# B of the state-space scan goes by DRAM and GpSimd, and the decays go to PSUM, in an eight-sequence sandwich kernel

## The chip, the cores and the metric

One core of a Trainium2 chip runs the whole kernel. The metric is device time in microseconds (us) of one execution; lower is better. Engines are TensorE (PE), VectorE (DVE), ScalarE (ACT), GpSimd (POOL) and SyncE (SP, which issues the DMAs here). Each works through its own instructions in order and waits on semaphores.

## What is computed

Eight sequences of 512 tokens, 256 wide, pass through two layers: attention, a routed mixture of eight small experts, a selective state-space block, and a ternary-weight feed-forward block, with norms and residual adds between them. The change touches the state-space block. For each of 512 inner channels and 16 states it runs a recurrence over the 512 tokens:

```
x, B, C, delta = projections of the hidden state
dA    = exp(delta * A)               # the decay, one per channel, state and token
state = dA * state + (delta * u) * B # B of a group of channels, state and token
y     = sum over the 16 states of state * C
```

B is shared by groups of 128 channels (64 rows in all: 4 groups of 16 states); C has 512 rows, one for every 16 channels and each state.

## The kernel before

**Staging.** Every sequence goes through three chains of steps: `early` (attention, gate), `late` (experts, norms, the projections of the state-space block, delta and du = delta * u), and, after the scan, `back` (gate by z, output projection, feed-forward block, store). The scan of a sequence has 64 tiles of 128 channels by 512 tokens, `PER = 64`: four channel tiles `ct` times 16 states `st`. An iteration runs the scan of sequence s and, woven into it, `late` of s+1, `early` of s+2 and `back` of s-1. The first iteration has no `back` chain of an earlier sequence, the second to last no `early`, and the last neither `early` nor `late`. A prologue with the first sequences' chains and an epilogue with the last `back` chain lie around the eight iterations.

**Order.** The order of each engine's work is fixed when the program is written out. `iteration` walks over steps j = -1 to 67 with three parts each (`SLOTS`), calls the scan function of the engine for (j, part), and then emits the chain steps that `in_slots` put into that slot; it spreads each chain's rounds by the planner's costs (`COST`). Within an engine nothing overtakes: a chain step that waits holds the scan work behind it.

**The scan of tile n in before** is made of these instructions, named by function:
- `scan_act`, part 0 of step n-1 (line 919): ScalarE writes decay(n) = exp(delta * a) into one of `NDA = 4` SBUF buffers, after scan n-4.
- `scan_pe`, part 1 of step n-1 (line 743): TensorE multiplies a one-hot selector (`sel_b`) by `b_rows` (B in three bf16 parts that add up to fp32) to spread row n of B over 128 partitions, into one of two PSUM banks `ps_b` (`NDB = 2`), after scan n-2.
- `scan_dve`, part 1 of step n (line 1210): VectorE multiplies that bank by du, in place.
- `scan_dve`, part 0 of step n+1 (line 1203): VectorE runs the recurrence, state(n) from decay and `ps_b`, into one of three state buffers (`NS = 3`), after product n-3.
- `scan_pool`, part 0 of step n+2 (line 1226): GpSimd multiplies state(n) by C from `c_all`, into one of four `prod` buffers.
- `scan_pe`, part 2 of step n+3 or n+4 (line 750): TensorE adds the product into `ps_y` by an identity matmul; after 16 tiles VectorE takes y out (line 1216).
- `scan_sync` (line 1308): one DMA of 256 KB for each tile loads C rows from DRAM, each row repeated over 16 partitions, into one of `NC = 5` buffers.

**Preparing B in before** (chain `late`): `bm` (24 small matmuls), `b_hi`, `b_rest`, `b_mid`, `b_lo` (ten VectorE instructions that split B into three bf16 parts), `b_turn` (8 transposes), `b_turned` (one ScalarE copy). x has a projection of its own, `xs`. C goes through `c`, `c_out`, `c_store` into DRAM.

Of the kernel before, what the change touches and what calls it, by code (L numbers as in the profile page):

```python
# [5 lines left out]
F32 = mybir.dt.float32  # L6
# [5 lines left out]
P = 128  # L12
# [36 lines left out]
C_BANK, CONV_BANK, D_BANK = (2, 1, 2, 0), (0, 2, 1, 0), (2, 1, 0, 2)  # L49
# [104 lines left out]
def late_rounds():  # L154

    steps = []
    for i in range(MCH):
        at, routed = 3 * i, i >= MCH - RCH
        steps += [(at, "P", ("up1", i)), (at + 1, "A", ("tanh", i)), (at + 1, "P", ("up3", i)), (at + 2, "V", ("silu", i))]
        if routed:  # L160
# [5 lines left out]
    steps = [(0, "P", "dt"), (0, "P", "bm"), (0, "V", "x4_zero"), (1, "A", "dt_out"), (1, "V", "b_hi"), (1, "P", ("c", 0)),  # L166
             (2, "V", "b_rest"), (2, "A", ("c_out", 0)), (3, "V", "b_mid"), (3, "P", ("c", 1)), (3, "S", ("c_store", 0)),
             (4, "V", "b_lo"), (4, "A", ("c_out", 1)), (4, "P", ("c", 2)), (5, "P", "b_turn"), (5, "A", ("c_out", 2)),
             (5, "S", ("c_store", 1)), (6, "A", "b_turned"), (6, "S", ("c_store", 2)), (6, "P", "xs"),
             (7, "P", ("c", 3)), (7, "A", ("x4", 0)), (8, "A", ("c_out", 3)),  # L170
             (9, "S", ("c_store", 3)), (9, "A", ("x4", 1)), (9, "P", ("conv", 0)),
             (10, "P", ("conv", 1)), (11, "P", ("conv", 2)), (13, "P", ("conv", 3))]
    for i in range(CT):
        steps += [(10 + i + (i == 3), "A", ("x_tanh", i)), (11 + i + (i == 3), "A", ("x_one", i)),
                  (12 + i + (i == 3), "V", ("u", i))]
    d0 = (14, 15, 17, 18)
# [38 lines left out]
def quant_rounds():  # L215
# [20 lines left out]
    "h_turned": 12, "dt": 15, "bm": 15, "dt_out": 7, "b_turn": 6, "b_turned": 12, "c": 15, "c_out": 7, "xs": 15, "x4": 24,  # L236
# [46 lines left out]
def sandwich(nc, base, wqT, bq, wkT, b_k, wvT, bv, woT, bo, gateT, gate_b, w1T, w3T, w2T, winT, wdtT, b_dt,  # L283
             conv_w, conv_b, a_log, d_param, woutT, w_fc, w_proj, ident, tri, sel_e, sel_n, out):
    c_rows = nc.dram_tensor("c_rows", [2, CT, P, T], F32).ap()
    ctx = ExitStack()
    with ctx:  # L287
# [26 lines left out]
        sel_b = sb("sel_b", [P, NST, 1], BF16)  # L314
# [12 lines left out]
        xn = sb("xn", [P, NT, D], BF16)  # L327
# [5 lines left out]
        b_rows = sb("b_rows", [P, 2, 2, T], BF16)  # L333
# [4 lines left out]
        NC, NDA, NDB, NS, NP = 5, 4, 2, 3, 4  # L338
        c_all = sb("c_all", [P, NC, T])
        decay = sb("decay", [P, NDA, T])  # L340
# [34 lines left out]
        bp = view(arena_l, 512, [NT, 2, 2, 64], BF16)  # L375
        br = view(arena_l, 1024, [NT, 64])
# [18 lines left out]
        win_f = c_all[:].rearrange("p a t -> p (a t)").rearrange("p (k n) -> p k n", k=KD)  # L395
# [27 lines left out]
        ps_b = ctx.enter_context(nc.psum_tensor("ps_b", [P, 2, T], F32))  # L423
# [11 lines left out]
        c_stored = [sem(f"c_stored{i}") for i in range(2)]  # L435
        out_stored = sem("out_stored")

        b_spread = sem("b_spread")
# [5 lines left out]
        y_taken = sem("y_taken")  # L444
        c_spread = [sem(f"c_spread{i}") for i in range(8)]
# [17 lines left out]
        ATTN_N, GATE_N, MOE_N, SSM_N = 8, 5, 4, 5  # L463
# [140 lines left out]
        def late_pe(eng, s, step):  # L604
# [38 lines left out]
            elif name == "bm":  # L643
                for t in range(NT):
                    n = 0
                    for part in range(3):
                        for k in range(KD):
                            ins = nc.tensor.matmul(ps_x[:, 1, t * 64:(t + 1) * 64],
                                                   hT[:, s.par, k, t * P:(t + 1) * P], win[:, k, part, BC:BC + 64],
                                                   start=(n == 0), stop=(n == 5))  # L650
                            n += 1
            elif name == "c":
                if i == 1:
                    eng.wait_ge(late["V"], la(s, "V", "b_rest"))
                elif i == 2:
                    eng.wait_ge(late["A"], la(s, "A", ("c_out", 0)))
                elif i == 3:
                    eng.wait_ge(late["A"], la(s, "A", "b_turned"))
                ins = project(ps_x[:, C_BANK[i], :], CC + i * P, P, hT[:, s.par])
            elif name == "b_turn":  # L660
                eng.wait_ge(late["V"], la(s, "V", "b_lo"))
                eng.wait_ge(late["A"], la(s, "A", "dt_out"))
                for pair in range(2):
                    for t in range(NT):
                        ins = nc.tensor.transpose(
                            xb(0)[:, pair * T + t * P:pair * T + (t + 1) * P],
                            bp[:, t, pair, :, :].rearrange("p a b -> p (a b)"), idb[:])
            elif name == "xs":
                eng.wait_ge(late["A"], la(s, "A", ("c_out", 1)))
                ins = project(ps_x[0:NXB * NST, 1, :], XC, NXB * NST, hT[:, s.par])  # L670
            elif name == "conv":
                if i == 0 and is_seq(s, 0):
                    eng.wait_ge(ready_conv, 1)
                eng.wait_ge(late["A"], la(s, "A", (("c_out", 3), ("c_out", 2), ("x4", 1), ("x4", 1))[i]))
                if i < 2:
                    eng.wait_ge(late["A"], la(s, "A", ("x4", 0)))
                elif i == 3:
                    eng.wait_ge(late["V"], la(s, "V", ("u", 0)))
# [56 lines left out]
        def scan_pe(eng, s, j, part):  # L735
            n = j + 1
            if part == 1 and 0 <= n < PER:
                if n == 0:
                    eng.wait_ge(late["A"], la(s, "A", "b_turned"))
                wait(eng, scanned, s.count(PER, n + 1 - NDB))  # L740
                ct, st = n // NST, n % NST
                lo = 64 * (ct % 2)
                nc.tensor.matmul(ps_b[:, n % NDB, :], sel_b[lo:lo + 48, st, :].broadcast_to([48, P]),  # L743
                                 b_rows[lo:lo + 48, s.par, ct // 2, :], start=True, stop=True).then_inc(b_spread, 1)
            if part == 2:
                for n in sums_at(j):
                    if n % NST == 0:
                        wait(eng, y_taken, s.count(PER, n))
                    eng.wait_ge(multiplied, s.count(PER, n + 1))
                    nc.tensor.matmul(ps_y[:], idf[:], prod[:, n % NP, :], start=(n % NST == 0),  # L750
                                     stop=(n % NST == NST - 1)).then_inc(reduced, 1)
# [60 lines left out]
        def late_act(eng, s, step):  # L812
# [21 lines left out]
            elif name == "b_turned":  # L834
                eng.wait_ge(late["P"], la(s, "P", "b_turn"))
                wait(eng, b_spread, s.count(PER, -PER))
                ins = nc.scalar.copy(b_rows[:, s.par], xb(0).rearrange("p (k t) -> p k t", k=2))
# [4 lines left out]
            elif name == "x4":  # L842
                eng.wait_ge(late["P"], la(s, "P", "xs"))
# [200 lines left out]
        def late_dve(eng, s, step):  # L1044
# [25 lines left out]
            elif i == "add":  # L1070
                eng.wait_ge(late["A"], la(s, "A", ("m", "apply")))
                wait(eng, back["G"], s.count(BPER, BACK_AT["G"][("w", "add")] - 2 * BPER))
                ins = tt(x2[:, s.par], x1[:, s.par], xn[:], ALU.add)
            elif name in ("silu", "weighted", "gated"):
# [11 lines left out]
                else:  # L1086
                    own(("silu" if shared else "weighted", i))
                    eng.wait_ge(late["P"], la(s, "P", ("up3", i)))
                    if i == 0:
                        for k in range(2):  # L1090
                            wait(eng, c_stored[k], s.count(PER, 0))
                    if shared:
# [6 lines left out]
            elif name == "b_hi":  # L1099
                eng.wait_ge(late["P"], la(s, "P", "bm"))  # L1100
                ins = nc.vector.tensor_copy(b_part(0), b_psum())
            elif name == "b_rest":
                own("b_hi")
                for t in range(NT):
# [518 lines left out]
```

## Time and profile before

| | us |
|---|---|
| time, median of 3 runs | 2097.96 (2095.51 to 2100.2) |
| the profiled execution's own time | 2099.33 |
| its span (first to last instruction) | 2097.5 |
| busy: PE / DVE / ACT / POOL | 1651.5 / 1770.0 / 1035.9 / 913.8 |

The page groups instructions by source line: busy time, count and mean duration, then how long the engine sat idle just before them and what ended that. Such idle time counts only where the engine is the one that sets the pace. A table of stretches gives the busy time of each engine in windows of the span, with the clock that TensorE was granted and the share of time that the 16 DMA engines were busy.

### The profile page before, as it was taken

What the parts mean: (1) busy time and instruction counts of PE and PEld (TensorE: products, weight loads), DVE (VectorE), ACT (ScalarE), POOL (GpSimd) and SP (SyncE); (2) the same over time, 40 slices, a digit from 0 to 9 for tenths busy, and PEclk for the clock granted to TensorE, in tenths of its full rate; (3) what the DMA queues carried; (4) which work ended last, traced back from release to release, by engine and by line L of the source; (5) the groups of instructions that cost most, each with busy time, mean ns of one, the idle gap of its engine ahead of it and who ended that gap; (6) DMA issues with size and microseconds to landing.
All of it is one profiled execution on the core that took longest, in us unless ns stands there. A gap on an engine that the chain in (4) does not pass through costs nothing. (4 is left out here: it accounts for less than half of the span.)

```text
span 2097.5 us, 22567 instructions
## 1 busy us (share of the span) xinstructions
PE 1651.5 (79%) x5875; PEld 725.3 (35%) x5948; DVE 1770.0 (84%) x3142; ACT 1035.9 (49%) x1745; POOL 913.8 (44%) x676
## 2 busy tenths in 40 slices
PE   3375577778996889868997799878997899779856
PEld 1122123232452335322452335332452335234324
DVE  6577899989879998979989998999989987987830
ACT  3247444825555454735556355734547344734312
POOL 0101534454437434554346434464346544665510
PEclk9977699979997999979997899979997899999978
DMA  4100222222222222222231222222222223223300
GB/s 108 46 0 21 72 79 89 92 69 77 75 92 65 85 71 86 85 67 78 74 101 65 81 76 76 96 75 72 76 96 71 76 85 106 86 99 113 110 10 11
DMA packets 94601, 157.95 MB, mean 75 GB/s; under 512 B 10940, under 2 KB 23660, under 8 KB 94468
## 3 DMA queue, kind: packets, MB, share of 16 engines
q1 hardware_dynamic: 94468, 156.43, 22.9%
q8 instruction: 52, 0.85, 0.2%
q14 instruction: 81, 0.66, 0.1%
HBM read 143.83 MB, written 12.58 MB: 75 GB/s over the span
## 5 line engine op out<-in xcount | busy, mean ns | idle before, releaser
L1226 POOL TENSOR_TENSOR prod<-state,c_all 128x512 f32<-128x512 f32 x512 | 669.6, 1312 | 706.8 <-DVE state L1203 644.0
L1203 DVE TENSOR_TENSOR_SCAN state<-decay,ps_b 128x512 f32<-128x512 f32 x512 | 619.7, 1210 | 9.7 <-issue 0.4
L750 PE MATMUL ps_y<-prod,idf 128*128 128x512 f32 x1024 | 610.6, 689 | 4.8 <-DVE u L1216 3.6
L1210 DVE TENSOR_TENSOR ps_b<-du,ps_b 128x512 f32<-128x512 f32 x512 | 347.7, 679 | 87.3 <-PE ps_b L743 86.8
L919 ACT ACTIVATE decay<-delta,a_neg 128x512 f32<-128x512 f32 x512 | 359.3, 719 | 32.3 <-DVE state L1203 29.3
L743 PE MATMUL ps_b<-b_rows,sel_b 48*128 48x512 bf16 x512 | 209.9, 411 | 155.0 <-DVE state L1203 152.7
L750 PEld LDWEIGHTS ps_y<-prod,idf 128*128 128x128 f32 x1024 | 183.8, 207 | 136.3 <-issue 109.9
L743 PEld LDWEIGHTS ps_b<-b_rows,sel_b 48*128 48x128 bf16 x512 | 47.8, 94 | 467.3 <-DVE state L1203 332.5
L619 PE MATMUL ps_x<-xT,w 128*128 128x512 bf16 (+1 forms) x391 | 132.0, 422 | 80.1 <-DVE arena_l L1095 65.6
L826 ACT ACTIVATE arena_l<-ps_x 128x512 f32<-128x512 f32 (+1 forms) x104 | 61.8, 594 | 190.8 <-PE ps_x L619 189.7
L535 PE MATMUL ps_x<-hT,win 128*128 128x512 bf16 (+1 forms) x455 | 135.6, 441 | 21.4 <-DVE arena_b L1171 16.6
L722 PE MATMUL ps_x<-arena_b,fcT 128*128 128x512 f32 x256 | 130.5, 634 | 6.0 <-ACT arena_b L901 4.8
L727 PE MATMUL ps_x<-pjT,arena_b 128*128 128x256 f32 x512 | 118.2, 384 | 3.1 <-ACT arena_b L907 1.7
L727 PEld LDWEIGHTS ps_x<-pjT,arena_b 128*128 128x128 f32 x512 | 95.3, 190 | 23.6 <-issue 6.4
L619 PEld LDWEIGHTS ps_x<-xT,w 128*128 128x128 bf16 (+1 forms) x416 | 32.4, 102 | 180.8 <-DVE arena_l L1095 104.9
L535 PEld LDWEIGHTS ps_x<-hT,win 128*128 128x128 bf16 (+1 forms) x480 | 48.5, 109 | 107.7 <-issue 44.3
L890 ACT ACTIVATE arena_b<-ps_x 128x512 f32<-128x512 f32 x32 | 19.0, 593 | 125.1 <-PE ps_x L535 125.1
L781 ACT ACTIVATE arena_e<-arena_e 128x512 bf16<-128x512 bf16 x64 | 39.6, 620 | 76.4 <-DVE arena_e L984 76.4
L901 ACT ACTIVATE arena_b<-ps_x 128x512 f32<-128x512 f32 x64 | 38.4, 599 | 75.0 <-PE ps_x L722 75.0
L1081 DVE SCALAR_TENSOR_TENSOR arena_l<-arena_l,ps_x 128x512 f32<-128x512 f32 (+1 forms) x104 | 69.9, 672 | 6.4 <-ACT arena_l L826 5.9
L711 PE MATMUL ps_x<-wout,u 128*128 128x256 f32 x256 | 61.9, 397 | 16.0 <-DVE u L1175 13.4
L722 PEld LDWEIGHTS ps_x<-arena_b,fcT 128*128 128x128 f32 x256 | 48.7, 200 | 65.4 <-issue 48.6
(230 smaller groups left out, 2422.2 us busy)
## 6 DMA issues: line engine op xcount, KB each, us to landing
c_all<-c_rows SPq DMA_DIRECT2D x512, 256.0 KB
c_rows<-arena_l SPq DMA_DIRECT2D x32, 256.0 KB
out<-arena_b SPq DMA_DIRECT2D x8, 512.0 KB
x_in<-in_base SPq DMA_DIRECT2D x8, 256.0 KB
c_all<-in_winT SPq DMA_DIRECT2D x1, 1280.0 KB, 7.5
arena_b<-in_w_fc SPq DMA_DIRECT2D x1, 1024.0 KB, 5.7
arena_b<-in_w_proj SPq DMA_DIRECT2D x1, 1024.0 KB, 5.0
w<-in_w1T SPq DMA_DIRECT2D x1, 792.0 KB, 5.9
```

What stands on the lines that cost most here:

```text
L535: ins = nc.tensor.matmul(dst, win[:, k, part, lo:lo + n], rhs[:, k, :], start=(i == 0), stop=(i == 5))
L619: ins = nc.tensor.matmul(ps_x[0:m, bank, :], w[:, k, c * P:c * P + m], xT[:, k, :], start=(k == 0), stop=(k == KD - 1))
L711: ins = nc.tensor.matmul(half_bank(XB, t), u[:, s.par, ct, t * P:(t + 1) * P], wout[:, ct, :], start=(ct == 0), stop=(ct == CT - 1))
L722: ins = nc.tensor.matmul(ps_x[:, XB, :], fcT[:, k, i * P:(i + 1) * P], x3T[:, k, :], start=(k == 0), stop=(k == KD - 1))
L727: ins = nc.tensor.matmul(ps_x[:, XB, 0:D], hf[:, m, i * P:(i + 1) * P], pjT[:, m, :], start=(m == 0), stop=(m == FM - 1))
L743: nc.tensor.matmul(ps_b[:, n % NDB, :], sel_b[lo:lo + 48, st, :].broadcast_to([48, P]), b_rows[lo:lo + 48, s.par, ct // 2, :], start=True, ...
L750: nc.tensor.matmul(ps_y[:], idf[:], prod[:, n % NP, :], start=(n % NST == 0), stop=(n % NST == NST - 1)).then_inc(reduced, 1)
L919: nc.scalar.activation(decay[:, n % NDA, :], delta[:, slot(s, ct), :], ACT.Exp, scale=a_neg[:, ct, st:st + 1]).then_inc(decayed, 1)
L1081: ins = stt(g, g, 1.0, ps_x[0:m, 0, :], ALU.add, ALU.mult)
L1203: nc.vector.tensor_tensor_scan(state[:, n % NS, :], decay[:, n % NDA, :], ps_b[:, n % NDB, :], 0.0, ALU.mult, ALU.add).then_inc(scanned, 1)
L1210: nc.vector.tensor_tensor(ps_b[:, j % NDB, :], du[:, slot(s, ct), :], ps_b[:, j % NDB, :], ALU.mult).then_inc(driven, 1)
L1226: nc.gpsimd.tensor_tensor(prod[:, n % NP, :], state[:, n % NS, :], c_all[:, n % NC, :], ALU.mult).then_inc(multiplied, 1)
```

## The change

**B** is projected together with x (`xb`, 128 rows in one go), ScalarE halves its 64 rows into an SBUF buffer (`b_out`), and one DMA stores them to a DRAM tensor `b_rows` (`b_store`). In the scan SyncE issues a second 256 KB load for each tile: one 2 KB row repeated over 128 partitions into one of `NB = 4` buffers `b_all`. GpSimd multiplies it by du into one of `NDB = 4` SBUF buffers `drive`, in step n-1, ahead of its product of tile n-3. The TensorE spread (line 743), the VectorE multiply (line 1210), `bm`, the five-step split, `b_turn`, `b_turned` and `xs` are gone.

**The decays** go from ScalarE into two PSUM banks (`NDA = 2`, before 4 in SBUF), so decay n waits for scan n-2. C has `NC = 4` buffers instead of 5, and its loads are issued from two steps on. The rounds of the last part of `late` are placed anew, the delta steps three rounds earlier.

```diff
-C_BANK, CONV_BANK, D_BANK = (2, 1, 2, 0), (0, 2, 1, 0), (2, 1, 0, 2)
+C_BANK, CONV_BANK, D_BANK = (2, 0, 2, 1), (0, 2, 1, 0), (2, 1, 0, 2)
...
+    steps = [(0, "P", "dt"), (0, "P", "xb"), (0, "V", "x4_zero"), (1, "A", "dt_out"), (1, "A", "b_out"), (1, "P", ("c", 0)),
+             (2, "P", ("c", 1)), (2, "S", "b_store"), (2, "A", ("c_out", 0)), (3, "A", ("x4", 0)), (3, "P", ("c", 2)),
...
-    d0 = (14, 15, 17, 18)
+        at = (6, 8, 10, 12)[i]
+        steps += [(at, "A", ("x_tanh", i)), (at + 1, "A", ("x_one", i)), (at + 2, "V", ("u", i))]
+    d0 = (11, 13, 15, 16)
...
-        NC, NDA, NDB, NS, NP = 5, 4, 2, 3, 4
-        c_all = sb("c_all", [P, NC, T])
-        decay = sb("decay", [P, NDA, T])
+        NB, NC, NDA, NDB, NS, NP = 4, 4, 2, 4, 3, 4
+        bc_all = sb("bc_all", [P, NB + NC, T])
+        b_all, c_all = bc_all[:, 0:NB], bc_all[:, NB:NB + NC]
+        drive = sb("drive", [P, NDB, T])
...
-        ps_b = ctx.enter_context(nc.psum_tensor("ps_b", [P, 2, T], F32))
+        decay = ctx.enter_context(nc.psum_tensor("decay", [P, NDA, T], F32))
...
+            elif name == "xb":
+                ins = project(ps_x[:, 1, :], XC, 2 * NXB * NST, hT[:, s.par])
...
         def scan_pe(eng, s, j, part):
-            n = j + 1
-            if part == 1 and 0 <= n < PER:
-                if n == 0:
-                    eng.wait_ge(late["A"], la(s, "A", "b_turned"))
-                wait(eng, scanned, s.count(PER, n + 1 - NDB))
-                ct, st = n // NST, n % NST
-                lo = 64 * (ct % 2)
-                nc.tensor.matmul(ps_b[:, n % NDB, :], sel_b[lo:lo + 48, st, :].broadcast_to([48, P]),
-                                 b_rows[lo:lo + 48, s.par, ct // 2, :], start=True, stop=True).then_inc(b_spread, 1)
...
+            elif name == "b_out":
+                eng.wait_ge(late["P"], la(s, "P", "xb"))
+                ins = act(bs[NXB * NST:P, :], ps_x[NXB * NST:P, 1, :], ACT.Copy, scale=0.5)
...
-                nc.vector.tensor_tensor_scan(state[:, n % NS, :], decay[:, n % NDA, :], ps_b[:, n % NDB, :], 0.0,
+                nc.vector.tensor_tensor_scan(state[:, n % NS, :], decay[:, n % NDA, :], drive[:, n % NDB, :], 0.0,
                                              ALU.mult, ALU.add).then_inc(scanned, 1)
-            if part == 1 and 0 <= j < PER:
-                ct = j // NST
-                if j % NST == 0:
-                    eng.wait_ge(late["G"], la(s, "G", ("du", ct)))
-                eng.wait_ge(b_spread, s.count(PER, j + 1))
-                nc.vector.tensor_tensor(ps_b[:, j % NDB, :], du[:, slot(s, ct), :], ps_b[:, j % NDB, :],
-                                        ALU.mult).then_inc(driven, 1)
...
         def scan_pool(eng, s, j, part):
+            n = j + 1
+            if part == 0 and 0 <= n < PER:
+                ct = n // NST
+                if n % NST == 0:
+                    eng.wait_ge(late["G"], la(s, "G", ("du", ct)))
+                eng.wait_ge(b_spread[n % 8], s.count(2 * PER, 16 * (n // 8 + 1)))
+                wait(eng, scanned, s.count(PER, n + 1 - NDB))
+                nc.gpsimd.tensor_tensor(drive[:, n % NDB, :], du[:, slot(s, ct), :], b_all[:, n % NB, :],
+                                        ALU.mult).then_inc(driven, 1)
...
+            if step == "b_store":
+                eng.wait_ge(late["A"], la(s, "A", "b_out"))
+                wait(eng, driven, s.count(PER, -PER))
+                eng.dma_start(b_rows[s.par], bs[NXB * NST:P, :]).then_inc(b_stored, PER)
+                return
...
-            for n in range(NC) if j == -1 else [j + NC - 1] if 1 <= j <= PER - NC else []:
+            for n in range(NB) if j == -1 else [j + NB] if 0 <= j < PER - NB else []:
                 stored = counted(eng, s.count(PER, PER)) if n == 0 else None
-                used = counted(eng, s.count(PER, n - NC + 1 if n >= NC else 0))
+                used = counted(eng, s.count(PER, n - NB + 1))
+                if n == 0:
+                    eng.wait_ge(b_stored, stored)
+                wait(eng, driven, used)
+                eng.dma_start(b_all[:, n % NB, :], b_rows[s.par, n:n + 1, :].broadcast_to([P, T])).then_inc(b_spread[n % 8], 16)
+            for n in range(NC) if j == -1 else [j + NC - 3] if 3 <= j <= PER - NC + 2 else []:
+                stored = counted(eng, s.count(PER, PER)) if n == 0 else None
+                used = counted(eng, s.count(PER, n - NC + 1))
```

## Rows read from the trace of the kernel before

**Rows 1.** Stretches by iteration: first, longest and shortest full one, last two.
```profile
231.50:452.70 221.20, 166.62 (x536) 60.53 (x546) 210.86 (x347) 109.66 (x181) 106.21 (x78) 0.86 0.25 84
...
690.80:932.70 241.90, 198.21 (x728) 89.04 (x737) 216.55 (x388) 127.43 (x217) 114.50 (x84) 0.92 0.24 80
...
1168.30:1403.90 235.60, 201.56 (x730) 89.51 (x739) 217.55 (x386) 127.35 (x217) 114.54 (x84) 0.91 0.24 80
...
1641.40:1849.50 208.10, 182.55 (x612) 79.79 (x618) 177.60 (x266) 105.65 (x171) 104.45 (x80) 0.94 0.27 88
1849.50:2002.70 153.20, 136.89 (x407) 59.89 (x407) 134.07 (x176) 61.48 (x101) 87.93 (x69) 0.97 0.33 111
```

**Rows 2.** The page's costliest groups: busy, mean ns of one, idle before, releaser.
```profile
L1226 POOL TENSOR_TENSOR prod<-state,c_all 128x512 f32<-128x512 f32 x512 | 669.6, 1312 | 706.8 <-DVE state L1203 644.0
L1203 DVE TENSOR_TENSOR_SCAN state<-decay,ps_b 128x512 f32<-128x512 f32 x512 | 619.7, 1210 | 9.7 <-issue 0.4
...
L1210 DVE TENSOR_TENSOR ps_b<-du,ps_b 128x512 f32<-128x512 f32 x512 | 347.7, 679 | 87.3 <-PE ps_b L743 86.8
L919 ACT ACTIVATE decay<-delta,a_neg 128x512 f32<-128x512 f32 x512 | 359.3, 719 | 32.3 <-DVE state L1203 29.3
L743 PE MATMUL ps_b<-b_rows,sel_b 48*128 48x512 bf16 x512 | 209.9, 411 | 155.0 <-DVE state L1203 152.7
```

**Rows 3.** Stretches of one full iteration, eight scan tiles each (columns as Rows 1).
```profile
1168.30:1195.70 27.40, 23.88 (x84) 10.60 (x83) 27.36 (x54) 12.66 (x22) 15.41 (x11) 0.94 0.25 84
1195.70:1223.40 27.70, 22.04 (x66) 7.63 (x66) 27.66 (x47) 13.44 (x24) 11.13 (x9) 0.88 0.23 77
1223.40:1251.00 27.60, 24.63 (x80) 9.48 (x80) 27.45 (x44) 16.43 (x32) 10.28 (x8) 1.00 0.25 76
1251.00:1280.50 29.50, 27.89 (x116) 14.03 (x116) 25.88 (x45) 17.31 (x33) 11.48 (x9) 1.00 0.23 75
1280.50:1307.20 26.70, 24.54 (x141) 15.68 (x144) 20.72 (x42) 13.34 (x23) 11.58 (x9) 1.00 0.24 80
1307.20:1335.00 27.80, 27.64 (x117) 14.86 (x117) 23.60 (x58) 13.99 (x25) 11.20 (x9) 1.00 0.35 111
1335.00:1363.20 28.20, 21.36 (x70) 7.03 (x68) 27.90 (x49) 23.62 (x40) 15.89 (x12) 0.87 0.22 74
1363.20:1403.90 40.70, 29.59 (x65) 10.19 (x67) 36.97 (x57) 16.56 (x23) 27.59 (x17) 0.67 0.21 66
```

**Rows 4.** Timeline of VectorE and GpSimd, 655 to 660 us: start, duration, instruction.
```profile
655.62 0.42 DVE L1121 TENSOR_SCALAR arena_l<-arena_l 128x512 f32<-128x512 f32 x1
...
657.15 1.27 POOL L1226 TENSOR_TENSOR prod<-state,c_all 128x512 f32<-128x512 f32 x1
657.69 0.68 DVE L1210 TENSOR_TENSOR ps_b<-du,ps_b 128x512 f32<-128x512 f32 x1
658.27 0.69 DVE L1175 TENSOR_TENSOR u<-u,arena_b 128x512 f32<-128x512 f32 x1
658.37 1.72 POOL L1248 TENSOR_TENSOR delta<-du,delta 128x512 f32<-128x512 f32 x1
658.88 1.76 DVE L1124 TENSOR_TENSOR arena_l<-arena_l 128x512 f32<-128x512 f32 x1
```

**Rows 5.** Two VectorE groups of the full iteration, columns as Rows 2.
```profile
L1121 DVE TENSOR_SCALAR arena_l<-arena_l 128x512 f32<-128x512 f32 x4 | 4.5, 1128 | 0.0
...
L1117 DVE SCALAR_TENSOR_TENSOR u<-ps_x,cb,u 128x512 f32<-128x512 f32 x4 | 2.9, 730 | 0.0
```

**Rows 6.** Three of GpSimd's 14 other groups of that iteration, columns as Rows 2.
```profile
L1248 POOL TENSOR_TENSOR delta<-du,delta 128x512 f32<-128x512 f32 x4 | 5.9, 1473 | 0.6 <-DVE du L1128 0.6
...
L1234 POOL TENSOR_TENSOR sd_x<-vb_x,hf 128x4 bf16<-128x4 bf16 x1 | 1.0, 1019 | 9.2 <-DVE vb_x L946 9.2
...
L509 POOL TENSOR_TENSOR rs_o<-ve_o,mhalf 128x4 f32<-128x4 f32 x1 | 1.0, 1007 | 3.9 <-DVE ve_o L1160 3.9
```

**Rows 7.** DMA issues: a load of 256 KB, median us from issue to landing.
```profile
wdt<-in_wdtT SPq DMA_DIRECT2D x1, 256.0 KB, 4.6
```

## What the change will do to the time, predicted before any run of it

> **What bounds the kernel now.** I read the table of stretches first, by iteration [rows 1]. Its columns are the stretch and its length, then the busy time of PE, weight loads, DVE, ACT and POOL, the granted TensorE clock, the DMA share and GB/s. The five full iterations take 235.6 to 241.9 us, and VectorE is busy for 217 of them, TensorE for 201, GpSimd for only 115. So VectorE is the pace, TensorE is close behind, and GpSimd is half idle. The last iteration is short, 153.2 us, because it has no early and late chains.
>
> Next the groups by line [rows 2]: per tile VectorE spends 1.210 us on the scan and 0.679 on the multiply by du, and nearly all of its idle time there (87.3 us) is ended by the TensorE spread of B, which itself waits for the scan two tiles back. GpSimd's product takes 1.312 us on average, nearly twice VectorE's time for the same form.
>
> Last, one full iteration cut into eight stretches of eight tiles [rows 3]. In stretches 1, 2, 3 and 7 VectorE is busy all the time (27.66 of 27.70). In 4 to 6 TensorE is (27.64 of 27.80). In the eighth nobody is full (36.97 of 40.70): it holds the delta steps, the gate and the passage to the next iteration. The busier of VectorE and TensorE sums to 227.5 us over the eight, against 235.6 measured: the in-order coupling costs 3.6%.
>
> **Part 1, VectorE loses the multiply.** Start to start it costs 0.58 us (657.69 to 658.27 [rows 4]; records overlap by 0.1), so 8 x 0.58 = 4.6 us per stretch and 37 per iteration. The split of B goes too (ten short instructions, about 3 us per iteration, in the late chain), and so does the wait for the spread, about 10 us per iteration; both are inside the stretch lengths, so I count them only through the maxima below. The same instruction exists only on GpSimd afterwards.
>
> **Part 2, GpSimd gains it.** The form is the one of its product: two fp32 SBUF inputs, 128x512. Back to back these cost 1.22 us (657.15 to 658.37 [rows 4]). Two of them per tile make 19.5 us per stretch and 156 per iteration. Its other work is its busy time less 8 x 1.31: 4.9, 0.6, 0, 1.0, 1.1, 0.7, 5.4 and 17.1 us in the eight stretches, 31 in all [rows 2, 3].
>
> **Part 3, the two engines exclude each other.** VectorE's multiply of two SBUF tensors at 658.88 took 1.76 us where its like took 0.69: GpSimd's instruction ran until 660.09, and VectorE ended 0.55 later. GpSimd's own, started at 658.37, took 1.72 instead of 1.27 behind VectorE's SBUF multiply of 658.27 [rows 4]. L1121 with a single SBUF source took 0.42 once and 1.128 on average [rows 5]. Instructions with a PSUM operand are not held, in either order of the operands: L1117, PSUM first and SBUF second, takes 730 ns evenly, like L1210 [rows 2, 5]. The new scan has this order too (decay in PSUM, drive in SBUF), so I leave it at 1.21; bounds 1.21 and, if it were held like the rest, 1.9. By the code a full iteration has about 93 VectorE instructions without a PSUM operand that are fit to be held, about 25 of them in the last stretch. GpSimd is busy half the time now and nearly always afterwards. I take 0.2 us more for GpSimd per such instruction (free durations 0.3 to 0.7, less overlap, less those that meet no one), 19 per iteration, 9 of it in the last stretch and 1.4 in each other; for VectorE 18 more waiting than now, 6 and 1.7. Bounds: 0 and twice that.
>
> The Trainium skill (SBUF — State Buffer, section "SBUF: two separate sides") puts this as an exclusive lock for the whole instruction. Taken to the letter, 128 full durations of 1.27 plus 31 plus some 30 of held VectorE work is 224 us of one port per iteration before any coupling, some 6 more than my sum. The trace agrees that they exclude each other, but back-to-back GpSimd instructions start every 1.22.
>
> **Part 4, TensorE** loses 8 x 0.411 = 3.3 us per stretch [rows 2] and some matmuls of the B preparation, which I count at nothing.
>
> **Part 5, ScalarE.** Decay n now waits for scan n-2, so it has one step (some 3.3 us) for 0.719 us of work [rows 2]. Behind it queue all chain steps of ScalarE; they come no earlier than the scan of their step. Cover: ScalarE is busy 127 of 236 us. Nothing for it; if every decay were exposed, 46 us per iteration. A write to PSUM instead of SBUF: no row, bounds -0.1 and +0.1 us, hidden.
>
> **Part 6, DMA.** C's loads keep the 16 DMA engines 0.24 busy [rows 1], that is 0.9 us per tile; B adds as much. B's load for tile n+4 may start when drive n is done and is wanted four steps later, some 13 us; a 256 KB load landed 4.6 us after its issue [rows 7]. C has one buffer fewer but still four steps. Hidden, and the b_store too, since B leaves far ahead of delta. On SyncE both loads stand in one queue with the chains' stores; a late store delays both by what it waits, with some 8 us of slack.
>
> **The sum for a full iteration**, largest of GpSimd (19.5 + other + held), VectorE (busy - 4.6 + held) and TensorE (busy - 3.3) [rows 3]: 25.8 (GpSimd), 24.8 (VectorE), 24.6 (VectorE), 24.6 (TensorE), 22.0 (GpSimd), 24.3 (TensorE), 26.3 (GpSimd), 45.6 (GpSimd: 19.5 + 17.1 + 9). That is 218.0 where it was 227.5. With 4% of coupling it gives 226.7 against 235.6: -8.9, five times -45. First iteration, with the lighter mix: -5. Second to last: GpSimd 156 + 21 + 8 = 185, plus its idle passage, about 200 against 208.1: -8. **Last iteration**: VectorE would need only about 100, but GpSimd 156 + 8 + 5 = 169, with coupling 173 against 153.2: +20. Prologue: -1. Together -39: 2099.3 - 39 = 2060 for the profiled execution, which lies 1.4 above the median of the runs; I predict 2060.
>
> **Rivals.**
> 1. *GpSimd turns into the pace and its waits come with it: slower.* GpSimd runs 13 chain instructions in an iteration (roots, deltas, adds) in order with drive and product. Its 14 other groups have 33 us of idle time before them now, from L1248's 0.6 to rs_o's 3.9 with sd_x's 9.2 between [rows 6]. Half idle, it doesn't feel them. If they stay, a full iteration needs 156 + 31 + 19 + 33 = 239 us, 3 more than the 235.6 now. Five of these make +15, the last iteration adds its +20, the first and the second to last stay: +35, 2134. It decides from about 20 us of such waits per iteration. For: in-order, and many waits for VectorE. Against: VectorE may run two steps ahead of a late GpSimd, so most predecessors will be done.
> 2. *TensorE's clock.* It was granted 1.00 (2.4 GHz) in the full stretches 4 to 6 and 0.67 in the last, where it was busy 29.59 of 40.70 us (a mix of both levels) [rows 3]. With 3.3 us less per stretch more of them may be granted less; then stretches 4 to 6 stay at 27.6 and the gain of 8 to 9 us per full iteration is gone: 2100. The Trainium skill's page TensorE: Matmul & The Clock Gate (section "HAM oscillation — how this bites in real kernels") describes a clock that is cut when the matmul stream pauses, and so speaks for this one.
> 3. *Loads late.* If one DRAM row read 128 times is slow (C reads eight rows), each tile waits; at 1 us a tile +512 us less the slack, at least 2200. No releaser of L1226 is a DMA now [rows 2].
> 4. *Couplings vanish*, as VectorE no longer waits for the spread: the full iterations come to 218, 17.6 less, total -88 - 13 + 18: 2015.
> That the change does not do what it says is not open: the instructions are in the diff.
>
> **How the numbers follow.** Forecast 0.50, rival 1 0.28, rival 2 0.09, rival 3 0.04, rival 4 0.09. The forecast's own range, from held time 0 to double (19 per full iteration either way, damped by VectorE-bound stretches to about 6), is 2025 to 2098. Range for 8 in 10: 2010 to 2135. No change is what a measurement cannot tell from 2098, within 0.2%, 4 us. Faster: 0.46 of the forecast, rival 4 and a third of rival 2, 0.58. Same: 0.03 of the forecast, 0.04 of rival 2 and 0.03 of rival 1, 0.10. Slower: the rest, 0.32.
>
> **What would show it.** GpSimd busy over 200 of a full iteration; VectorE near 190; the last iteration near 173 us and full of GpSimd; the scan at 1.21 us still; VectorE's SBUF instructions longer (L1121 over 1.2 us); no wait of GpSimd for a DMA. It would be wrong if GpSimd idles over 20 us per full iteration waiting for VectorE (rival 1), if the scan is longer than 1.3 us, or if ScalarE's decay is what the scan waits for.

## The result, and the profile after

The changed kernel takes 2110.64 us (median of 7 runs, 2104.84 to 2121.6); the kernel before takes 2098.19 (2095.51 to 2100.28). The ratio is 1.0064, 95% interval 1.004 to 1.0088: slower by 0.6%, where I forecast 2060, faster by 1.8%. The measured time lies in the range that I gave, and the sign is wrong. The profiled execution took 2104.84 us with a span of 2103.0; it is the fastest of the seven, so the trace shows 5.5 of the 12.5 us between the medians.

The page's groups that answer to [rows 2] (busy us, mean ns, idle before, releaser):

```profile
L1177 POOL TENSOR_TENSOR prod<-state,bc_all 128x512 f32<-128x512 f32 x512 | 673.6, 1316 | 165.9 <-DVE state L1152 143.8
L1152 DVE TENSOR_TENSOR_SCAN state<-decay,drive 128x512 f32<-128x512 f32 x512 | 618.6, 1211 | 91.9 <-POOL prod L1177 64.8
...
L1170 POOL TENSOR_TENSOR drive<-du,bc_all 128x512 f32<-128x512 f32 x512 | 670.2, 1310 | 10.9 <-issue 5.5
L887 ACT ACTIVATE decay<-delta,a_neg 128x512 f32<-128x512 f32 x512 | 352.4, 691 | 633.2 <-DVE state L1152 624.4
```

The scan still takes 1.211 us, and the multiply, now on GpSimd, 1.310. New are the 633 us that ScalarE idles before its decays, nearly all of it waiting for the scan; before it was 32.3 us.

The stretches that answer to [rows 1]: first iteration, the five full ones together, second to last, last. Columns: stretch, length, busy PE, weight loads, DVE, ACT, POOL, granted clock, DMA share, GB/s. First the kernel before, whose five full iterations did not stand in one row yet, then the changed one.

```profile
452.70:1641.40 1188.70, 1007.43 (x3647) 449.19 (x3695) 1084.20 (x1919) 636.97 (x1085) 572.60 (x420) 0.91 0.24 78
```

```profile
228.50:450.20 221.70, 142.54 (x447) 56.34 (x446) 193.76 (x274) 112.45 (x183) 185.98 (x143) 0.80 0.54 164
450.20:1647.20 1197.00, 897.73 (x3215) 440.17 (x3214) 1045.30 (x1548) 653.88 (x1095) 979.58 (x741) 0.86 0.49 149
1647.20:1841.90 194.70, 156.79 (x523) 77.37 (x521) 142.79 (x192) 106.63 (x171) 182.17 (x144) 0.92 0.58 179
1841.90:2011.70 169.80, 123.72 (x347) 58.99 (x348) 110.58 (x114) 62.88 (x102) 161.98 (x131) 0.86 0.62 189
```

Where the 5.5 us come from: the five full iterations +8.3 (239.4 us each, before 237.7), the last +16.6, the second to last -13.4, the prologue -3.0, the epilogue -3.5, the first +0.5. The two last iterations came out near the forecast (+20 and -8). The full iterations, where I had expected -45, gained nothing, although neither VectorE (209.1 us each, 87%) nor GpSimd (195.9, 82%) nor TensorE (179.5, 75%) is full.

One full iteration of the changed kernel in eight stretches of eight scan tiles, columns as above, to be set beside [rows 3]:

```profile
1176.90:1207.50 30.60, 23.16 (x79) 11.31 (x78) 28.83 (x47) 12.92 (x22) 22.84 (x19) 0.89 0.45 134
1207.50:1233.10 25.60, 17.72 (x58) 6.71 (x57) 24.43 (x39) 13.65 (x24) 23.55 (x19) 0.93 0.55 166
1233.10:1260.90 27.80, 23.01 (x77) 9.40 (x76) 27.61 (x37) 16.63 (x32) 20.77 (x17) 1.00 0.52 156
1260.90:1289.00 28.10, 23.27 (x99) 13.49 (x100) 22.87 (x37) 17.36 (x33) 21.44 (x17) 0.88 0.53 153
1289.00:1314.40 25.40, 25.40 (x132) 17.27 (x131) 16.72 (x28) 12.62 (x23) 20.70 (x17) 1.00 0.54 165
1314.40:1336.30 21.90, 20.58 (x90) 12.66 (x89) 21.27 (x46) 14.73 (x25) 20.40 (x16) 1.00 0.68 217
1336.30:1368.00 31.70, 19.35 (x70) 8.02 (x68) 26.73 (x41) 22.74 (x35) 26.26 (x21) 0.87 0.47 148
1368.00:1412.50 44.50, 23.20 (x48) 7.69 (x49) 38.51 (x48) 20.00 (x28) 39.99 (x26) 0.63 0.39 115
```

In stretches 4, 7 and 8 no engine is full: 28.10 us with 23.27 of the busiest, 31.70 with 26.73, 44.50 with 39.99.

So the account of VectorE is what has to be explained. Per full iteration it was busy 216.8 us and idle 20.9; it is now busy 209.1 and idle 30.3. The multiply and the split took 40 away, so 177 were to be expected before any longer holding: **busy is 32 us above that**. And the idle time changed hands. Its waits in the five full iterations, first of the kernel before, then of the changed one (us in total, times, longest):

```profile
DVE ps_b L1210 <- PE ps_b L743: 51.7, 36, 4.1
DVE st_m L497 <- PE ps_x L633: 18.2, 10, 3.0
DVE u L1216 <- PE ps_y L750: 18.1, 5, 3.8
```

```profile
DVE g L965 <- ACT g L771: 24.2, 5, 4.8
DVE arena_e L937 <- ACT arena_e L759: 23.7, 5, 4.8
DVE arena_e L945 <- ACT arena_e L746: 21.7, 10, 3.1
DVE arena_b L1120 <- ACT arena_b L858: 15.7, 5, 3.2
DVE state L1152 <- ACT decay L887: 14.5, 10, 1.9
...
DVE arena_l L1049 <- ACT arena_l L795: 9.8, 10, 3.4
...
DVE state L1152 <- POOL prod L1177: 5.0, 5, 1.2
```

For TensorE it waits 4.8 us per iteration instead of 17.6, for ScalarE 22.2 instead of 0.8. All rows of ScalarE but the `decay` row are waits for **chain steps** of ScalarE, not for the decays. For GpSimd VectorE waits only 1.2 us per iteration.

Both can be seen in one place, in the 1176.9 to 1412.5 iteration (start, duration, engine, instruction):

```profile
1181.67 4.08 DVE L919 TENSOR_SCALAR arena_e<-x_in,mb_x 128x256 bf16<-128x256 bf16 x4
1185.67 1.21 DVE L1152 TENSOR_TENSOR_SCAN state<-decay,drive 128x512 f32<-128x512 f32 x1
```

```profile
1181.95 1.26 POOL L1170 TENSOR_TENSOR drive<-du,bc_all 128x512 f32<-128x512 f32 x1
1183.18 1.26 POOL L1177 TENSOR_TENSOR prod<-state,bc_all 128x512 f32<-128x512 f32 x1
1184.41 1.26 POOL L1170 TENSOR_TENSOR drive<-du,bc_all 128x512 f32<-128x512 f32 x1
```

```profile
1181.41 0.69 ACT L887 ACTIVATE decay<-delta,a_neg 128x512 f32<-128x512 f32 x1
1186.92 0.69 ACT L887 ACTIVATE decay<-delta,a_neg 128x512 f32<-128x512 f32 x1 [4.82 <-DVE state L1152]
1187.55 0.58 ACT L795 ACTIVATE arena_l<-ps_x 128x512 f32<-128x512 f32 x1
```

Four short norm instructions of VectorE, free 0.27 us each, take 4.08 us together: 0.41 the first, 1.30 each of the others. GpSimd has its next instruction ready at each turn here, and the two engines alternate: one norm instruction, one GpSimd instruction. GpSimd isn't slowed by it, its instructions still start every 1.23 us. The scan behind them starts only at 1185.67; ScalarE's next decay waits for it, 4.82 us; and the chain step behind the decay, the tanh of L795, comes only then.

This is the worst case, not the rule. Of the 30 such bursts of four in the five full iterations, 14 had three or four instructions held (over 0.9 us each), nine had one or two, and seven none. Together the bursts take 19.1 us per full iteration, where the kernel before has 9.1, so they are 10 of the 32 us. Nor is it always GpSimd that wins. In the kernel before, at the same place:

```profile
1173.06 1.98 DVE L951 TENSOR_SCALAR arena_e<-x_in,mb_x 128x256 bf16<-128x256 bf16 x4
```

```profile
1171.32 3.64 POOL L1226 TENSOR_TENSOR prod<-state,c_all 128x512 f32<-128x512 f32 x2
```

Here three norm instructions pass at 0.27 us each while the second product, started at 1172.54, takes 2.42 us instead of 1.27; only the fourth is held (1.39). What decides who is first is not shown.

### The profile page after: what moved, and what is told of

Its sections match the earlier page's. It is cut to its first block and busy times, and to the rows that moved or that the text cites. A ratio compares the mean times of both kernels' runs of the same rounds, so it can differ in the third digit from the quotient of the medians.

```text
span 2103.0 us, 22040 instructions
## 1 busy us (share of the span) xinstructions
PE 1473.4 (70%) x5180; PEld 706.9 (34%) x5180; DVE 1652.5 (79%) x2550; ACT 1056.6 (50%) x1757; POOL 1555.2 (74%) x1188
## 5 line engine op out<-in xcount | busy, mean ns | idle before, releaser
L1177 POOL TENSOR_TENSOR prod<-state,bc_all 128x512 f32<-128x512 f32 x512 | 673.6, 1316 | 165.9 <-DVE state L1152 143.8
L1152 DVE TENSOR_TENSOR_SCAN state<-decay,drive 128x512 f32<-128x512 f32 x512 | 618.6, 1211 | 91.9 <-POOL prod L1177 64.8
L1170 POOL TENSOR_TENSOR drive<-du,bc_all 128x512 f32<-128x512 f32 x512 | 670.2, 1310 | 10.9 <-issue 5.5
L719 PEld LDWEIGHTS ps_y<-prod,idf 128*128 128x128 f32 x1024 | 204.4, 217 | 326.3 <-POOL prod L1177 183.7
L533 PE MATMUL ps_x<-hT,win 128*128 128x512 bf16 x480 | 142.9, 447 | 102.7 <-DVE arena_b L1120 93.4
L533 PEld LDWEIGHTS ps_x<-hT,win 128*128 128x128 bf16 x480 | 49.6, 109 | 207.6 <-DVE arena_b L1120 119.0
L795 ACT ACTIVATE arena_l<-ps_x 128x512 f32<-128x512 f32 (+1 forms) x104 | 61.1, 587 | 51.0 <-PE ps_x L617 50.7
L1188 POOL TENSOR_TENSOR g<-g,half 128x32 f32<-128x32 f32 x8 | 45.7, 5712 | 28.9 <-DVE g L975 28.9
L709 PEld LDWEIGHTS ps_x<-arena_b 128*128 128x128 f32 x512 | 61.8, 192 | 9.3 <-issue 8.1
L1053 DVE TENSOR_TENSOR arena_l<-arena_l,ps_x 128x512 f32<-128x512 f32 x88 | 59.1, 671 | 4.5 <-PE ps_x L625 2.5
L709 PE MATMUL ps_x<-arena_b 128*128 128x128 f32 x512 | 62.3, 275 | 0.0
```

The costliest lines, as they stand in the source:

```text
L533: ins = nc.tensor.matmul(dst, win[:, k, part, lo:lo + n], rhs[:, k, :], start=(i == 0), stop=(i == 5))
L709: ins = nc.tensor.matmul(ps_x[:, XB, D:D + P], hf[:, m, i * P:(i + 1) * P], hf[:, m, i * P:(i + 1) * P], start=(m == 0), stop=(m == FM - 1))
L1152: nc.vector.tensor_tensor_scan(state[:, n % NS, :], decay[:, n % NDA, :], drive[:, n % NDB, :], 0.0, ALU.mult, ALU.add).then_inc(scanned, 1)
L1170: nc.gpsimd.tensor_tensor(drive[:, n % NDB, :], du[:, slot(s, ct), :], b_all[:, n % NB, :], ALU.mult).then_inc(driven, 1)
L1177: nc.gpsimd.tensor_tensor(prod[:, n % NP, :], state[:, n % NS, :], c_all[:, n % NC, :], ALU.mult).then_inc(multiplied, 1)
```

## The experiments

Three theories. **A:** the two decay buffers hold ScalarE's chain steps behind the scan. **B:** GpSimd and VectorE exclude each other instruction by instruction, so bursts of short VectorE instructions pay a whole GpSimd instruction each. **C:** TensorE's lower granted clock (0.857, before 0.899) eats the gain, rival 2 of the prediction.

Ratios are to the kernel before, measured beside each group of runs. Its median was 2094.86 to 2098.99 us there and the changed kernel was measured only with the first, so differences in us between medians of different groups can be off by some 4 us.

### e1 and e4: ScalarE's decay is emitted later

```diff
         def scan_act(eng, s, j, part):
             n = j + 1
-            if part == 0 and 0 <= n < PER:
+            if part == 2 and 0 <= n < PER:
```

> Changed kernel with ScalarE's decay of tile n emitted in part 2 of step n-1 instead of part 0, so that its wait for scan n-2 holds fewer chain steps of ScalarE. Theory A (the two PSUM buffers tie ScalarE to the scan, its chain steps come late and VectorE waits for them, 22 us of idle time per full iteration): VectorE's idle time ended by ScalarE falls from 22 to under 10 us per full iteration, and the time from 2110 to 2030 to 2060. Theory B (the port that GpSimd and VectorE share costs the time, VectorE is longer busy): idle time moves into lock time or waits for GpSimd, 2095 to 2110.

Measured: 2082.26 us, ratio to before 0.9931 (0.9914 to 0.9948), 28 us under the changed kernel and 0.7% under the kernel before. e4 puts the decay yet one part later (`n = j`, part 0):

> Changed kernel with ScalarE's decay of tile n emitted in part 0 of step n instead of step n-1 (one part later than in e1), where scan n-2 is always done before. Theory A: ScalarE no longer waits for the scan at all (76 us of its idle time per full iteration in the changed kernel, 40 in e1, now under 15) and its chain steps come in time; 2060 to 2080. Against it: the scan of tile n has only one step for its decay, and VectorE's waits for the decay itself (2.9 us per full iteration, 5.5 in e1) grow; if these win, 2085 to 2110.

Measured: 2079.12 us, 0.9931 (0.991 to 0.9953), the same as e1. The full iterations fall from 239.4 to 233.7 (e1) and 234.7 us (e4):

```profile
446.80:1615.50 1168.70, 891.57 (x3215) 438.56 (x3214) 1050.53 (x1549) 648.71 (x1095) 978.20 (x741) 0.86 0.49 153
```

VectorE's busy time is unchanged (210.1 each), its idle time falls by 6.7. The time is less than expected of theory A, and so is the cause: VectorE waits for ScalarE still 17 us per full iteration in e1, where I had expected under 10. ScalarE's own wait before the decays (whole run; changed kernel, e1, e4):

```profile
ACT decay L887 <- DVE state L1152: 624.4, 340, 8.8
```
```profile
ACT decay L887 <- DVE state L1152: 374.2, 204, 11.6
```
```profile
ACT decay L887 <- DVE state L1152: 273.1, 136, 8.8
```

The held time falls, but even in e4 it is 29 us per full iteration (76 in the changed kernel, 40 in e1), where I had expected under 15. My reading, which no run tests, is that ScalarE, busy 129 of 235 us, catches up with VectorE wherever the decay stands. The price of the shift shows too: the scan waits more for the decay itself, 37.6 us in e1 and 53.3 in e4, 26.9 in the changed kernel.

### e2: the kernel before with two decay buffers

```diff
-        NC, NDA, NDB, NS, NP = 5, 4, 2, 3, 4
+        NC, NDA, NDB, NS, NP = 5, 2, 2, 3, 4
```

> Kernel before with two SBUF buffers for the decays instead of four, nothing else. Theory A: the same coupling appears alone, VectorE idles for ScalarE where it did not (0.9 us per full iteration before), and the time rises by 60 to 120 us. Theory B: within 10 us of before, since nothing of the port changes.

Measured: 2140.67 us, 1.0204 (1.0187 to 1.0221), +42 us. Theory A holds by sign, its size was overrated. This is the price of that one number with nothing else changed. ScalarE's wait is that of the changed kernel:

```profile
ACT decay L919 <- DVE state L1203: 642.9, 351, 9.0
```
```profile
DVE g L997 <- ACT g L802: 32.9, 8, 5.8
```

VectorE's waits for ScalarE are the same in kind, but not in size: 5.8 us per full iteration, where the kernel before has 0.8 and the changed one 22.2. The full iterations are 5.5 us longer (243.3). So the two buffers alone explain 5 of the 21 us by which these waits grew; why the changed kernel has so many more is not shown. The new places of `late`'s rounds came with the change and were not run alone.

### e3: GpSimd's multiply on 64 of 512 columns

```diff
-                nc.gpsimd.tensor_tensor(drive[:, n % NDB, :], du[:, slot(s, ct), :], b_all[:, n % NB, :],
+                nc.gpsimd.tensor_tensor(drive[:, n % NDB, 0:64], du[:, slot(s, ct), 0:64], b_all[:, n % NB, 0:64],
...
+            nc.vector.memset(drive[:], 0.0)
```

> Changed kernel in which GpSimd multiplies only 64 of the 512 columns of each drive tile (the rest of drive stays zero, so this part of the computation is left out); all waits and loads stay. It takes some 0.9 us per tile off GpSimd and off its hold on the port. Theory B: VectorE's held instructions get back to their durations of before, about 30 us less per full iteration, time 1920 to 1980. Theory A alone: VectorE still idles 20 us per full iteration for ScalarE, the full iterations keep over 225 us, and only the last two shrink: 2050 to 2080.

Measured: 1953.42 us, 0.9306 (0.9289 to 0.9323). GpSimd's instruction takes 357 ns instead of 1310. The full iterations (1097.4 / 5 = 219.5 us):

```profile
428.60:1526.00 1097.40, 868.75 (x3216) 436.31 (x3215) 904.09 (x1548) 652.89 (x1095) 667.19 (x741) 0.90 0.55 162
```

VectorE is busy 180.8 us, 28 less with the same instructions: these 28 are holding by GpSimd. The time lies where theory B had it; a full iteration is 20 us shorter, not the 30 expected. Not all of the 20 need be holding, since the edit also takes 62 us of GpSimd's own work out of each full iteration. Theory A is seen beside it: VectorE still waits 29 us per full iteration for ScalarE.

### e9: e1 and e3 together

> Changed kernel with both e1 (decay two parts later) and e3 (GpSimd multiplies 64 of 512 columns of each drive tile, the rest left out). If the two losses are separate, their gains add: 1953 - 28 = 1925, full iterations near 212 us. If they are one loss seen twice (VectorE waits for ScalarE only because GpSimd holds VectorE), the second adds little: 1945 to 1955.

Measured: 1907.56 us, 0.9102 (0.9088 to 0.9116), under both expected values. The later decay is worth 46 us here, not 28. So the two losses are not one loss seen twice. They seem to hide part of each other: VectorE's waits for ScalarE grew from 22 to 29 us per full iteration when GpSimd held it less (e3).

### e5 and e6: four norm instructions in one

```diff
+        def per_row(v):
+            return v[:].rearrange("p (t o) -> p t o", o=1).broadcast_to([P, NT, D])
...
-                for t in range(NT):
-                    ins = ts(xe[:, t, :], xe[:, t, :], ri[name][:, t:t + 1], None, ALU.mult)
+                ins = tt(xe, xe, per_row(ri[name]), ALU.mult)
```

> Changed kernel in which each of the six norm steps of the early chain that is four VectorE instructions of 128x256 bf16 (centre, divide) is one instruction of 128x1024 with a broadcast operand; same result. Theory B (GpSimd and VectorE take the shared port in turn, one instruction each, so a burst of four is held four times at some 1.0 us): one hold instead of four, VectorE's busy time falls by 8 to 12 us per full iteration, time 2050 to 2085. If a burst were held only once, as my forecast counted, the merged form gains nothing: 2105 to 2120.

> Kernel before with the same merged norm steps as e5. There GpSimd is half idle and holds bursts less, so both theories expect little: 2090 to 2110; it tells what part of e5's gain is the merged form by itself.

Measured: e5 2089.57 us, 0.9971 (0.9959 to 0.9983), 21 us under the changed kernel; e6 2101.86, 1.0028 (1.0017 to 1.004), some 5 us **over** the kernel before. The same edit gains in the changed kernel alone. In e6 the full iterations stay as they were (237.6 us, before 237.7), and the time is added ahead of them: 2.8 us in the prologue, 1.7 in the first iteration. One of the six steps in the kernel before, in the changed one and in e5 (whole run, busy and mean ns):

```profile
L958 DVE TENSOR_SCALAR arena_e<-arena_e,ri_y 128x256 bf16<-128x256 bf16 x32 | 13.3, 475 | 0.1
```
```profile
L926 DVE TENSOR_SCALAR arena_e<-arena_e,ri_y 128x256 bf16<-128x256 bf16 x32 | 28.0, 937 | 0.1
```
```profile
L928 DVE TENSOR_TENSOR arena_e<-arena_e,ri_y 128x1024 bf16<-128x1024 bf16 x8 | 13.7, 1717 | 0.1
```

This is the step that is held most. A burst of four costs 4 x 937 ns, one instruction with four times the data 1717. The merged form isn't free of cost: its shortest takes 1201 ns, where four free short ones take some 0.9 us, and GpSimd is busy 5 us more per full iteration in e5. VectorE's busy time in the full iterations falls by 6.5 us each, less than the 8 to 12 expected.

### e7: the changed kernel with more matmuls

```diff
+        zero = sb("zero", [48, P], BF16)
...
+                    if n % NST < NST - 1:
+                        nc.tensor.matmul(ps_y[:], zero[:], win[0:48, 0, 0, 0:T], start=False, stop=False)
...
+            nc.vector.memset(zero[:], 0.0)
```

> Changed kernel with one more TensorE matmul per tile (zero weights, added into ps_y, 15 of 16 tiles), about as much work as the removed spread of B. Theory C (TensorE's granted clock, 0.857 here and 0.899 before, is what cost the gain): the clock comes back to about 0.90 and the time falls to 2075 to 2095. Theories A and B: TensorE isn't the pace, the time stays or rises a little, 2108 to 2130.

Measured: 2161.35 us, 1.0301 (1.027 to 1.0332). The granted clock came back only from 0.857 to 0.869, and the time rose by 51 us, more than any theory said. The full iterations:

```profile
454.40:1684.70 1230.30, 1006.82 (x3466) 441.41 (x3514) 1044.56 (x1547) 655.26 (x1095) 978.94 (x741) 0.88 0.47 145
```

TensorE has 22 us more per full iteration and the iteration is 6.7 longer. This does not test theory C as I meant it, for the clock hardly rose: 0.88 in the full iterations, where the kernel before has 0.91. Against theory C speak two other things. Of the stretches 4 to 6, which rival 2 had standing at 27.6 us, only the fourth did (28.10, 25.40, 21.90 above); and e10 below reaches 228.3 us per full iteration at a granted clock of 0.860, as low as the changed kernel's 0.857. So the gain could be had without the clock. What the lower clock costs by itself is not shown. What e7 does show is that TensorE's work is not as free as "not the pace" suggested.

### e8: in the last iteration VectorE takes every third multiply

```diff
+            n = j + 1
+            if part == 1 and 0 <= n < PER and on_dve(s, n):
...
+                nc.vector.tensor_tensor(drive[:, n % NDB, :], du[:, slot(s, ct), :], b_all[:, n % NB, :],
+                                        ALU.mult).then_inc(driven_v, 1)
...
+        def on_dve(s, n):
+            return is_seq(s, NBATCH - 1) and n % 3 == 2
```

> Changed kernel in which, in the last iteration alone, VectorE makes every third drive tile (21 of 64) from the same SBUF operands, and GpSimd the rest. The forecast's reading of the last iteration (GpSimd is the pace at 156 us of work, 169.8 measured, VectorE a third idle): GpSimd gives up 21 x 1.22 = 26 us and is held some 10 us by the moved ones, so the last iteration falls to 150 to 156 us and the time to 2088 to 2100. If the last iteration were paced by something else, it stays at 168 to 172.

Measured: 2097.47 us, 0.9999 (0.9977 to 1.002), 13 us under the changed kernel. The last iteration falls from 169.8 to 150.6 us, as expected of a stretch that GpSimd paces:

```profile
1852.10:2002.70 150.60, 120.62 (x345) 60.52 (x346) 124.86 (x134) 62.28 (x102) 145.91 (x110) 0.86 0.67 213
```
```profile
L1161 DVE TENSOR_TENSOR drive<-du,bc_all 128x512 f32<-128x512 f32 x21 | 29.5, 1403 | 0.0
```

VectorE pays 1403 ns for each, twice the free 690, and could afford it there.

### e10 and e11: the three together

e10 is the changed kernel with e1, the merged norm steps (not for the first two sequences, whose early chains run in the prologue, without GpSimd's scan work) and e8; e11 has e4 in place of e1.

> Changed kernel with the decay two parts later (e1), the norm steps of all but the first two sequences merged (e5) and a third of the last iteration's drives on VectorE (e8). If theories A and B and the reading of the last iteration hold and add: 2110 - 28 - 24 - 16 = 2042, range 2030 to 2060.

> The same with the decay one step later (e4) instead: within 8 us of e10, 2030 to 2062.

Measured: e10 2036.84 us, 0.9722 (0.9709 to 0.9735); e11 2041.11, 0.9739 (0.9719 to 0.9759). Both beat both kernels; e10 is 2.8% faster than the kernel before. Together the three edits give 74 us, where 68 were expected (28 + 24 + 16) and the edits alone gave 62 (28 + 21 + 13). The full iterations take 228.3 us each, close to the 226.7 that I had predicted for the change as it was:

```profile
445.80:1587.50 1141.70, 878.23 (x3215) 431.06 (x3214) 1027.03 (x1458) 649.39 (x1095) 1005.47 (x741) 0.87 0.50 156
```

## Why the prediction was wrong

**What held.** The reading of the ends: last iteration 173 forecast, 169.8 measured; second to last 200 and 194.7. The prices of the moved instruction (1.22 us start to start), the scan at 1.21 with its operands exchanged, L1121's successor over 1.2 us on average, loads that hide (GpSimd waited 5.4 us in the whole run for B's load) all came out. GpSimd is busy 195.9 us per full iteration; my terms gave 206 (156 + 31 + 19), so its holding by VectorE was some 9 us, not 19.

**Part 5 failed.** I priced the two decay buffers at nothing, naming as cover that ScalarE is busy only 127 of 236 us. The cover of the decays was indeed good (the scan waited only 2.9 us per full iteration for one). What I named and did not price was the other half of that sentence, the chain steps queued behind the waiting decay. Idle share is no cover for a queue: VectorE's waits for ScalarE went from 0.8 to 22.2 us per full iteration. e2 gives that edit's price in the kernel before, 42 us, 5.5 of them per full iteration; in the changed kernel e1 gives back 28 us, 5.7 per full iteration, by a mere move. By e2 the buffers alone account for 5 of those 21 us of waits; the rest is open.

**Part 3 was mis-sized.** The mechanism was right, but for VectorE I took 18 us more per full iteration and it was 32 (28 of them vanish in e3). The 32 lie within the bounds that I gave, 0 and twice 18. I had averaged a hold over single instructions, although [rows 4] showed each engine, once waiting, to be next. Where GpSimd has its next instruction ready, a burst is held again and again: 4.08 us for four of 0.27. The Trainium skill (SBUF — State Buffer, section "SBUF: two separate sides"), which I had set beside the sum, says that whichever engine starts first keeps the shared port for its whole instruction. By that rule I had worked out 6 us more per iteration for GpSimd's side of the port; the measured surplus of VectorE was 14. The trace agrees that the two exclude each other (1.30 us for a norm instruction that takes 0.27 free), but not on the order: in the burst of 1173.06 above the product had started first and three norm instructions passed it. What e5 adds, measured, is that a burst pays for its count: one merged instruction was held for less than four.

**The coupling term.** I took 3.6% from the kernel before and raised it to 4%. The 3.6% came from one iteration of 235.6 us, one of the two shortest. Over all five, the busiest engine of each stretch of eight tiles sums to 227.4 us of 237.7, and the coupling is 4.6%. In the changed kernel the same sum is 220.1 us, only 2 over my 218.0, but the full iteration takes 239.4: 8.8%, 19.3 us where I had added 8.7. So of the 12.7 us by which I missed, 2 lie in the sum of the stretches and the rest in the coupling. My reading, not shown by a run of its own, is that the mis-sized holding hurts less by its length than by what comes late behind it, which my sum had no term for. By the same measure e2 has 6.4%, e1 7.0% and e10 6.2%.

**The rivals.** Rival 1 had the sign and, with 239 us, the length of a full iteration (239.4); by 2134 it missed the total, as it gave the second to last iteration nothing, which gained 13.4. The sign that I had set for it came too: GpSimd idles 43.5 us per full iteration, 35 of them for VectorE, where over 20 was to speak for rival 1. Its mechanism came only in part. Some 17 of the 43.5 lie before chain steps, where it had 33 (and 20 chain instructions by [rows 3], not the 13 that I wrote), and 26 before products. GpSimd is the pace in the last iteration (e8), and at most in stretch 8 of a full one, for over a whole full iteration VectorE waits only 1.2 us for it. Rival 2 said that stretches 4 to 6 would stay at 27.6 us; two of the three did not, and e10 has the gain at the low clock. The Trainium skill (TensorE: Matmul & The Clock Gate, section "HAM oscillation — how this bites in real kernels"), which spoke for that rival, has the clock cut when the matmul stream pauses. The trace agrees in direction: with less matmul work the grant is lower (0.86 against 0.91 in the full iterations). What that cost is not shown. Rival 3 did not occur; only in e3, with shorter steps, does GpSimd wait 53.7 us for the loads of C. Rival 4 was the opposite of the truth: the coupling grew.

**Open.** e1 removed 5.7 of the 12.7 us per full iteration by which I missed, e5 another 3.9. VectorE still waits 17 us per full iteration for ScalarE in e1; which order of ScalarE's steps would remove that was not tried. Nor were the new places of `late`'s rounds and C's four buffers run alone. Why e7 costs 51 us with TensorE at 82% is not settled either. Four decay buffers in the changed kernel, which would test Part 5 most directly, were not tried; in SBUF they would give the scan two SBUF operands.

## What to carry to other kernels

When a buffer count falls, ask who stands in the queue behind the new wait, not how busy the waiting engine is; moving the waiting instruction later in its own queue gave back 28 us here. When work moves from VectorE to GpSimd, look at VectorE's bursts of short instructions without a PSUM operand. One GpSimd instruction for each is the upper bound, reached in some bursts; over all of the some 93 such instructions of a full iteration the surplus was 32 us, 0.34 each. Merging a burst paid here and did not pay in the kernel before (e5 -21 us, e6 +5 us). A sum over the busiest engines can be right, as it was here, and the time still wrong: what has to be priced then is what each engine's queue waits for. Read an engine's slack stretch by stretch: the same move cost 16.6 us in the last iteration and gained 13.4 in the one before.

## What the runs showed of the hardware

GpSimd and VectorE hold each other on their SBUF work, in the worst bursts instruction by instruction: four VectorE instructions of 0.27 us took 4.08 us beside back-to-back GpSimd instructions of 1.26, which weren't slowed. It is not strict: seven of 30 such bursts were not held at all, and in one of the kernel before three passed during a GpSimd product, which took 2.42 us instead of 1.27. A 128x512 fp32 multiply of VectorE from SBUF took 1403 ns on average, where it has 0.69 free. A scan with its first input in PSUM and its second in SBUF takes 1.211 us beside a GpSimd that is busy 82% of a full iteration, as it does with the two exchanged and GpSimd half idle (1.210). ScalarE's exponential of 128x512 takes 691 ns into PSUM and 719 into SBUF. Loads of one 2 KB row repeated over 128 partitions landed 4.4 us after their issue (median).
